# Loads, fills and stores of the first batch laid out anew, and router logits computed turned, in an attention and mixture-of-experts kernel

## The reference, cut to what matters

```python
x = x + attn(layernorm(x));  x = x + ffn(layernorm(x))

# attn
Q, K, V = (x @ W + b for ...)                       # 16 heads of 16
attn = softmax(causal(Q @ K.T) * scale)             # exact maximum per row
h = layernorm(x @ dp_w1 + dp_b1) * ln_g + ln_b      # 128 wide
drift = gelu(h) @ dp_w2 + dp_b2
gate = tanh(gelu(drift * g_w1 + g_b1) @ g_w2 + g_b2)  # one number per token
out = (attn * gate) @ V ... @ Wo + bo

# ffn, 8 experts of 128, 2 chosen per token, and a shared part of 2 x 128
logits = x @ gate_w.T;  scores = sigmoid(logits)    # group-limited choice of 2
y = sum over chosen experts of w2 @ (silu(w1 @ x) * (w3 @ x)) * weight;  + shared(x)
```

## Time and profile before

| | |
|---|---|
| runs | 1950.63, 1959.01, 1960.4 us; median 1959.01 |
| profiled execution, its span | 1949.71 us, 1947.7 us |
| PE matmul, busy | 1735.7 us, 89% |
| PE weight load, busy | 1069.2 us, 55% |
| DVE, ACT, POOL, busy | 67%, 56%, 39% |

### The profile page before, as it was taken

One profiled execution on the slowest core, in us unless ns is written; L12 is line 12 of the kernel. 1 busy time (PEld: TensorE's weight loads), 2 busy tenths in 40 slices (PEclk: granted clock), 3 DMA queues, 4 the chain that ended last, 5 costly groups with the idle time before them and its releaser, 6 DMA issues.

```text
span 1947.7 us, 39672 instructions
## 1 busy us (share of the span) xinstructions
PE 1735.7 (89%) x13066; PEld 1069.2 (55%) x13066; DVE 1302.9 (67%) x2546; ACT 1094.8 (56%) x1822; POOL 763.4 (39%) x1110
## 2 busy tenths in 40 slices
PE   3489889979999899988999899989999889988997
PEld 1244446535665556545665456645665456646786
DVE  1387676866678666866768666776668667763564
ACT  1436755565555754567555774567555665566342
POOL 4422422262115732177214752166321772155151
PEclk8679899979999999989999799998999889988999
DMA  7555353354435555356445464355552563336131
GB/s 237 171 130 141 99 164 99 97 150 118 130 92 164 165 145 155 104 160 187 130 131 157 131 188 122 101 172 150 153 148 86 168 184 100 93 104 191 48 110 41
DMA packets 194881, 263.67 MB, mean 135 GB/s; under 512 B 19712, under 2 KB 129408, under 8 KB 194688
## 3 DMA queue, kind: packets, MB, share of 16 engines
q1 hardware_dynamic: 183936, 231.77, 40.8%
q0 software_dynamic: 10752, 29.37, 5.3%
HBM read 134.13 MB, written 126.35 MB: 134 GB/s over the span
## 4 chain that ended last, share of the span: by engine, by line
PE 61%; DMA 10%; issue 7%; ACT 7%; DVE 6%; POOL 5%; SPq 4%; POOLq 0%; ACTq 0%; DVEq 0%
PE ps_all L1634 12%; PE ps_all L1728 12%; PE ps_all L1582 7%; PE ps_all L1754 6%; PE ps_all L1614 6%; DMA qk_s<-ql 4%; PE ps_all L1566 4%; ACT probs L1137 4%; DVE mx L1282 3%; PE ps_all L1552 3%; PE ps_all L1642 3%; PE ps_all L1667 2%; PE ps_all L1738 2%; PE ps_all L1689 1%; PE ps_all L1589 1%
## 5 line engine op out<-in xcount | busy, mean ns | idle before, releaser
L1282 DVE TENSOR_REDUCE mx<-ps_all 128x2 f32<-128x1024 f32 (+2 forms) x640 | 619.9, 1004 | 124.9 <-PE ps_all L1582 67.4
L1137 ACT ACTIVATE probs<-ps_all 128x1024 f32<-128x1024 f32 x576 | 574.4, 1027 | 214.7 <-PE ps_all L1614 209.6
L1582 PE MATMUL ps_all<-k_st,q_st 48*128 48x512 f32 (+3 forms) x1536 | 309.9, 430 | 71.4 <-DVE mx L1282 22.1
L1634 PE MATMUL ps_all<-probs,vaug 128*32 128x512 f32 (+3 forms) x3072 | 339.6, 538 | 24.0 <-POOL probs L984 16.3
L984 POOL TENSOR_SCALAR_AFFINE_SELECT probs<-probs 128x512 f32<-128x512 f32 x256 | 161.4, 645 | 488.5 <-ACT probs L1137 487.5
L1614 PE MATMUL ps_all<-q_st,k_st 49*128 49x512 f32 (+3 forms) x1536 | 266.5, 401 | 35.5 <-ACT probs L1137 20.5
L1582 PEld LDWEIGHTS ps_all<-k_st,q_st 48*128 48x128 f32 x1536 | 160.0, 197 | 196.9 <-issue 81.4
L1614 PEld LDWEIGHTS ps_all<-q_st,k_st 49*128 49x128 f32 x1536 | 136.1, 194 | 157.7 <-issue 69.6
L1728 PE MATMUL ps_all<-w_hi,x2h 128*128 (+1 forms) x528 | 190.8, 361 | 9.4 <-DVE x2l L1331 4.7
L1728 PE MATMUL ps_all<-w_lo,x2h 128*128 (+1 forms) x528 | 176.4, 334 | 0.0
L1728 PE MATMUL ps_all<-w_hi,x2l 128*128 (+1 forms) x528 | 175.7, 333 | 0.0
(11 more groups left out here) (162 smaller groups left out, 3041.2 us busy)
## 6 DMA issues: line engine op xcount, KB each, us to landing
qk_s<-qh SPq DMA_DIRECT2D x128, 256.0 KB
q_st<-qk_s SPq DMA_DIRECT2D x128, 192.0 KB, 4.1
k_st<-qk_s SPq DMA_DIRECT2D x128, 192.0 KB, 4.8
xs<-xs_s SPq DMA_DIRECT2D x84, 256.0 KB
ys_s<-ysb SPq DMA_DIRECT2D x84, 256.0 KB
qk_s<-ql SPq DMA_DIRECT2D x64, 256.0 KB
o_s<-o_sb SPq DMA_DIRECT2D x64, 256.0 KB, 3.3
xa<-in_x SPq DMA_DIRECT2D x32, 256.0 KB, 3.2
```

Of the source, the lines that this page charges most:

```text
L1137: nc.scalar.activation(to, of, ACT.Exp, scale=DH ** -0.5).then_inc(freed[release[item][0]], 1)
L1282: last = nc.vector.tensor_reduce(to[:, :, p, qt % QPC], both[:, :, at:at + keys], X_AXIS, ALU.max)
L1582: last = mm(bank(item, j)[:, to:to + keys], q_st[r, q_half(n, g, c), p, qt % QPC * P:(qt % QPC + 1) * P], k_st[r, k_half(n, g, kc), p, 0:k ...
L1634: last = mm(bank(first)[32 * h:32 * h + 32, q0 - c * CHUNK:], vaug[:, kt, g, h * VW:h * VW + 32], probs[:, s % 2, h, at:at + cols], start= ...
```

## The change

- SP loads the first two parts of x first; the weights are two items (`WL` 0 for values, `WL` 1 for queries and keys), the small constants and `Wo` an item `WC`, `turn_bars` an item `BT`.
- The fill with ones of `k_st` is cut into five items on POOL (`PK` 0 to 4), that of `vaug` and the small constants are two more; so the normalisation of x can run between them.
- The zeros of the slots are written in 12 transfers of 512 KB (`XZ`), planned from 100,000 ns on, one each 20,000 ns. The six loads of expert weights are planned from 110,000 ns on, one each 20,000 ns, and not earlier (`early`).
- In batch 0 each unit v has its own place for the high and the low part (tiles of later stages, still free, are borrowed) and its own semaphore `first_st[v]`. Only the second half of the batch waits for the stores of the first.
- `CG` holds `gate_w` (128 by 8) as weights and moves 256 tokens: 6 matmuls for a quarter. The logits come out turned, 8 by 256. `CI` takes their tanh on ACT into `logits_t`, `CJ` turns it back on PE with two transposes, and `RT` becomes a copy. The wait for the routing of the batch before moves from `CG` to `RT`.
- Planned lengths and landing times for batch 0 are made smaller, and `FIRST` is 50,000.

```diff
-FIRST = 75_000
+FIRST = 50_000
...
             add("SP", ("AX", n, h), ISSUE, due - 12000, [("AN", n - (h < 2), (h - 2) % HALVES * QT + QT - 1)],
-                lands=4500)
+                lands=4500 if n else 2600)
+            if n == 0 and h < 2:
+                add("SP", ("WL", h), 1800, due, lands=3000)
...
-                    before = [("SQ",) + unit(i - 1)] if i else []
-                    if i > 1:
-                        before.append(("SQ",) + unit(i - 2))
+                    before = [("SQ",) + unit(i - k) for k in ((1, 2) if n else (4,)) if i >= k]
...
-        add("PE", ("CG", n, q), 1400, pre + 14000, low + [("RO", n - 1, ROUTE_OPS - 1)], 1, FULL)
-        add("ACT", ("RT", n, q), 200, pre + 14000, [("CG", n, q)], frees=(("CG", n, q), None))
+        add("PE", ("CG", n, q), 750, pre + 14000, low, 1, FULL)
+        add("ACT", ("CI", n, q), 390, pre + 14000, [("CG", n, q), ("CJ",) + prev])
+        add("PE", ("CJ", n, q), 250, pre + 15000, [("CI", n, q)], 0, FULL)
+        add("ACT", ("RT", n, q), 200, pre + 15000, [("CJ", n, q), ("RO", n - 1, ROUTE_OPS - 1)], frees=(("CG", n, q), None))
...
-        add("SP", ("WF", i), ISSUE, 60000 + 9000 * i, [("WP", i - 1)], lands=5500)
-        add("ACT", ("WH", i), 1300, 60000 + 9000 * i, [("WF", i)])
-        add("POOL", ("WP", i), 2900, 60000 + 9000 * i, [("WH", i)])
+        begin = 110_000 + 20_000 * i
+        add("SP", ("WF", i), ISSUE, begin, [("WP", i - 1)], lands=5500, early=begin)
+        add("ACT", ("WH", i), 1300, begin + 6000, [("WF", i), ("WC",)])
+        add("POOL", ("WP", i), 2900, begin + 8000, [("WH", i)])
+
+    def constants():
+        for k in range(K_HALVES + 2):
+            ns, due = (1000, 5000 + 1500 * k) if k < K_HALVES else (2400, 25000) if k == K_HALVES else (2200, 30000)
+            add("POOL", ("PK", k), ns, due, early=5500 if k < K_HALVES else due)
+        add("SP", ("BT",), 1300, 6000, lands=3000, early=5000)
+        add("SP", ("WC",), 3400, 14000, lands=4000, early=14000)
+        for k in range(2 * CLEARS):
+            begin = 100_000 + 20_000 * k
+            add("SP", ("XZ", k), ISSUE, begin, [("PK", K_HALVES + 1)], lands=6000, early=begin)
...
+        def high_of(n, v):
+
+            if n or v < 2:
+                return qh[:, v % 2, :]
+            return xs[:, v % 2, :, :].rearrange("p t e -> p (t e)").bitcast(F32R)
+
+        def low_of(n, v):
+            if n or v == 0:
+                return ql[:]
+            place = rr[:] if v == 3 else yab[:, v - 1, :, :]
+            return place.rearrange("p a e -> p (a e)").bitcast(F32R)
...
                 for kind in range(2):
-                    sp.wait_ge(qh_st[kind], done * 32)
+                    if n:
+                        sp.wait_ge(qh_st[kind], done * 32)
+                    else:
+                        sp.wait_ge(first_st[2 * m + kind], (c + 1) * 48)
                     fence(sp)
...
+                for k in range(KE):
+                    for t, (xx, w) in enumerate(((x2h, gw_hi), (x2h, gw_lo), (x2l, gw_hi))):
+                        last = mm(bank(item)[0:EXPERTS, 0:Q], w[:, k, :], xx[:, buf, k, :],
+                                  start=(k == 0 and t == 0), stop=(k == KE - 1 and t == 2))
+                last.then_inc(cg_full, 1)
+
+            def turn_logits(item, n, q):
+                pe.wait_ge(cg_tanh, n * QS + q + 1)
                 for i in range(QT):
-                    ts = slice(i * P, (i + 1) * P)
-                    for k in range(KE):
-                        for t, (xx, w) in enumerate(((x2h, gw_hi), (x2h, gw_lo), (x2l, gw_hi))):
-                            last = mm(bank(item)[:, i * EXPERTS:(i + 1) * EXPERTS], xx[:, buf, k, ts], w[:, k, :],
-                                      start=(k == 0 and t == 0), stop=(k == KE - 1 and t == 2))
-                last.then_inc(cg_full, 1)
+                    last = nc.tensor.transpose(bank(("CG", n, q))[:, Q + i * EXPERTS:Q + (i + 1) * EXPERTS],
+                                               logits_t[0:EXPERTS, i * P:(i + 1) * P], ident[0:EXPERTS, 0:EXPERTS])
+                last.then_inc(cj_full, 1)
```

More of the change, by code:

```diff
@@ L68 @@
 FFN_CHUNKS = 6
+CLEARS = 6
 HALVES = TILES // QT
@@ L153, in __init__, with add @@
     def __init__(self):
-        self.items, self.queues, self.place, self.spaced = {}, {}, {}, {}
-    def add(self, engine, item, ns, due, after=(), banks=0, tiling=None, frees=None, lands=None, spaced=None):
+        self.items, self.queues, self.place, self.spaced, self.early = {}, {}, {}, {}, {}
+    def add(self, engine, item, ns, due, after=(), banks=0, tiling=None, frees=None, lands=None, spaced=None, early=0):
         self.items[item] = (engine, ns, due, [a for a in after if a in self.items], banks, tiling, frees, lands)
+        self.early[item] = early
         if spaced and spaced[0] in self.items:
@@ L301, in gate @@
         add("ACT", ("GC", n), 2300, due, [("GB", n)])
-        add("POOL", ("GD", n), 4800, due, [("GC", n)])
+        add("POOL", ("GD", n), 4800, due, [("WC",), ("GC", n)])
         add("ACT", ("GE", n), 3600, due, [("GD", n)])
@@ L312, in values @@
     def values(n, g):
-        add("POOL", ("VA", n, g), 2000, at(n, g) - 4000, [("GL", n), ("PV", n - 1, g, NSTEP - 1)])
+        add("POOL", ("VA", n, g), 2000, at(n, g) - 4000, [("PK", K_HALVES), ("GL", n), ("PV", n - 1, g, NSTEP - 1)])
     def maxima(n, g):
@@ L439, in routing @@
         for i in range(2 * TILES):
-            add("POOL", ("SX", n, i), 1250, begin + 14000 + 500 * i, [("RO", n, INDEX_OP)], lands=4000,
+            add("POOL", ("SX", n, i), 1250, begin + 14000 + 500 * i, [("RO", n, INDEX_OP)] + [("XZ", n * CLEARS + k) for k in range(CLEARS if n < 2 else 0)], lands=4000,
                 spaced=(("SX", n, i - 1), SCATTER_APART))
@@ L455, in pair @@
         expert(n, QS, u, due, [("XO", n, u), ("RO", n, TILE_OP)])
-        add("ACT", ("YC", n, u), 600, due + 3500, [("ED", n, QS, u)] + ([("YS",) + divmod(k - 1, SLOT_PAIRS)] if k else []),
+        add("ACT", ("YC", n, u), 600, due + 3500, [("ED", n, QS, u)] + ([("YS",) + divmod(k - 1, SLOT_PAIRS)] if k else [("XZ", 2 * CLEARS - 1)]),
             frees=(("ED", n, QS, u), None))
@@ L488, in rest @@
             pair(n, u)
+    constants()
     for n in range(B):
@@ L641, in build @@
         qh_st = [sem(f"qh_st{i}") for i in range(2)]
+        first_st = [sem(f"first_st{i}") for i in range(2 * KE)]
         g_dve, g_pool, g_act, g_mean = sem("g_dve"), sem("g_pool"), sem("g_act"), sem("g_mean")
@@ L907, in _, with constants @@
             nc.gpsimd.tensor_copy(bars[:, 0, 1, :], causal).then_inc(bars_set, 1)
[L908 to L917 removed]
+            def constants(item, k):
+                if k < K_HALVES:
+                    nc.gpsimd.memset(k_st[:, k, :, :].bitcast(F32), 1.0).then_inc(ones_set, 1)
+                elif k == K_HALVES:
+                    nc.gpsimd.memset(vaug[:], 1.0).then_inc(ones_set, 1)
+                else:
+                    nc.gpsimd.memset(ysb[:, 0, :], 0.0).then_inc(ones_set, 1)
+                    for i in range(EXPERTS):
+                        nc.gpsimd.memset(fills[:, i:i + 1], float(i * P))
+                    for i in range(SLOT_TILES):
+                        nc.gpsimd.memset(tile_no[:, i:i + 1], float(i))
+                    for one in scan:
+                        nc.gpsimd.memset(one[:, 0:PAD, :], 0.0)
+                    nc.gpsimd.memset(ones[:], 1.0).then_inc(ones_set, 1)
             def rstd_a(item, n, h):
@@ L1006, in scatter_tile @@
                 pool.wait_ge(route, routed(n, INDEX_OP))
-                if n == 0:
-                    pool.wait_ge(xs_clear, 32)
-                elif n >= 2:
+                if n < 2:
+                    pool.wait_ge(xs_clear[n], CLEARS * 16)
+                else:
                     for b in range(2):
@@ L1189, in copy_slots @@
                 if k == 0:
-                    act.wait_ge(xs_clear, 32)
+                    for i in range(2):
+                        act.wait_ge(xs_clear[i], CLEARS * 16)
                 else:
```

141 lines of the change are left out of this document (76 added, 65 removed).

## The result

Twenty runs of the kernel after have a median of 1939.15 us (1926.96 to 1956.09), twenty of the kernel before 1950.62 (1942.7 to 1960.4). The ratio is 0.9939, 95% interval 0.9918 to 0.9959: faster by 12 us, clear of noise but well under 2%. The prediction, a ratio of 0.972 and 1904 us, was wrong: some 43 us of the forecast gain didn't come, and the time lies above its range of 1884 to 1934. The profiled execution took 1940.05 us (span 1938.3).

The account below looks back on a forecast made before the run. PE was taken as the bound, after a beginning under half load: 1949.7 - 50 (beginning) - 9.6 (logits) + 5 (zeros, expert weights) = 1895.1 us profiled, ratio 0.972, median 1904; range 1884 to 1934.

Parts of the forecast that it names:

- PE starts at 7.3, second statistics before 6: Start of the kernel: PE begins 3.65 us after x at 3.63; DVE does the second statistics before 6 us.
- I take 50: Beginning, up to batch 0's first sums: 50 us saved of a computed 54, bounds 28 to 54.
- rival A: Beginning stays half serial: 15 to 20 us lost, first sums at 81 to 86, median 1919 to 1924; chance 0.17.
- The marker: Batch 0's first sums (first `PV`), at 120 us before, forecast at 66; taken as the same state in both kernels.
- From there on PE is full: After the first `PV` at 120.04 us PE is full, so that time was taken as the marker.
- Logits, -9.6: Gate logits on PE: 0.40 us saved for each of 32 quarters, 12.8 us, three quarters counted; bounds -12.8 and 0.
- rival B: Start is won, but waits replace PE's saved logits work: logits 0, median 1914, up to 1930; chance 0.08.
- I take three quarters: Share of the 12.8 us saved on PE's logits counted to the end, from chain share 61% and load 92%.
- Zeros and expert weights, +5: Both moved under batch 0's attention: cost of 5 us together, as DMA and POOL are more than half idle.
- rival C: `WF` loads hold SP in the attention, waiting for `WP`: at 12 us each of six, median 1971; chance 0.04.
- Due times, 0, 10 each way: Smaller `FIRST` moves all later due times alike: cost 0, with 10 us each way for the order made anew.
- The other 1828 us stay 92% busy: Rest of the kernel after the first 120 us: PE's load there stays 92%, as before.

Follow-up runs that it names:

- e2: Kernel after with the turned logits undone (logits computed as before), on two chips: 0.9923 and 0.9946 of the kernel before.
- e6: Kernel after with the expert weight loads back at their old, early due times: 0.9928 of the kernel before.
- e5: Kernel after with batch 1's x loaded from 62 us, batch 0's stores planned to land in 7 us, its gate due earlier: 0.9935 and 0.9916 of the kernel before.
- e10: Kernel after with the six logits matmuls of each quarter done twice, same order: 0.9987 of the kernel before.
- e3: Kernel after with the zero transfers planned later, from 265 us on, 8 us apart: 0.9971 of the kernel before.
- e11: e5, turned logits kept, but planned at the old logits' length of 1400 ns: 0.9907 of the kernel before.
- e8: e5 with the old logits in place of the turned ones, timed three times: 0.9833, 0.9863 and 0.9892 of the kernel before.
- e12: e8, old logits kept, but planned at the new logits' length of 750 ns: 0.988 of the kernel before.
- e4: Kernel after with 28 filler matmuls on PE in its wait for the second half's stacks: 0.9924 of the kernel before.

## Why the prediction was wrong, by its own steps

- **PE starts at 7.3, second statistics before 6:** right, 7.71, and all four at 3.83 to 5.3.
- **"I take 50" for the beginning:** this step failed, in two ways. First in its parts. PE's projection work was taken without gaps, to 42, and the data to be ready by 61; DVE stood behind x of batch 1, a store of SP's landed in 9.7, and the last stacks of that stage came at 59.2 with their maxima still to do. The gate went behind maxima: rival A, with first sums at 85.2 as it had it (81 to 86), though its time, 1919 to 1924, was wrong too. The marker moved by 34.8, within the bounds of 28 to 54, and at 85.2 it is just past the 85 that the prediction named as a sign of being wrong; a landing of low parts is still on the chain. Then in its meaning: "From there on PE is full" made each us of the marker a us of the end. Of 34.8 there were 14.1 left at the first sums of batch 1, and 10 to 15 at the end (e2). The work that had stood idle at a low clock now ran at that low clock (17.7 us), and no term of the sum had the clock in it. e6 moved the marker by 13 with no effect at the end, e5 moved the next one by 9 to 17 with almost none.
- **Logits, -9.6:** the matmuls were sized right (0.40 us saved a quarter, 12.8 in all; from start to next start it is 26.8 + 7.1 = 33.9 us for 32, where it was 46.9 before, 13.0 less) and `CJ` hardly waits, as forecast. The worth was wrong: 0 here, as rival B had it, and a loss in the repaired start, which nothing had. The step that failed is that the saving at the logits was taken for a saving of PE: of 12.5 us at one clock 4 are left in PE's sum, and that is less than these timings can tell from nothing. Rival B had waits in the place of saved work; the waits only moved. "I take three quarters" isn't refuted by e10, which gives half, with 2 to 19 us of 22.7.
- **Zeros and expert weights, +5:** nearer to 0. No wait of SP for `WP` is seen in the kernel after, rival C had nothing; e3 and e6 won nothing by moving them.
- **Due times, 0, 10 each way:** nothing speaks against it. `FIRST` at 65,000 (e9) changed nothing, and kernels that differ in one planned length only (e5 and e11, e8 and e12) are about 3 us apart, within the scatter.
- **"The other 1828 us stay 92% busy":** 1526 + 159 of 1853 us behind the first sums, 91%. One point there is 19 us, and a busy share at a low clock isn't work done.
- Sum by what was measured, to the end: start -14 at batch 1, of which -10 to -15 is left at the end (e2 twice: 0.9923, 0.9946), logits 0, the rest 0. That is the 12 us measured.

The range failed since its high end, 1934, like the worst case behind it, 1936 by the prediction's own sum, had the worst start and 0 for the logits and then still counted every us of the marker.

## What to carry to other kernels

Before a gain at the start is counted to the end, look for a second marker later on and ask what the engines do between the two: idle time at a low clock that is filled with work at that low clock is won only by half. A saving on the busiest engine is to be looked for in that engine's whole work, at one clock and each us counted once: here a third of it was left, and it gave nothing. Try each part of a change alone, and together with the next one: without its turned logits this one, with the order of the start repaired, was 0.4 to 1% faster than as it was made, though either step taken alone gave nothing that shows.

## What the runs showed of the hardware

- PE's granted clock was at its lower level from 56.5 to 100.9 us, after PE had been idle since 51.5, and stayed there with PE busy 71%, then 91% by the rows. In e4 it fell at 67.8, 3 us behind 12.25 us in which PE was busy without a gap at 1.00. The Trainium skill, "TensorE: Matmul & The Clock Gate", its part on the clock gate, has the clock follow how busy PE has been; the rows of the filler agree; those of 78 to 101 us don't, if busy is read off the matmul rows. What kept the clock low there wasn't settled.
- Time goes with the mean granted clock of a run. Of the kernel after, a run at 0.939 took 1926.96 us, one at 0.923 1951.23; over the twenty runs it is 1.4 us for 0.001. Sets in which the kernel before ran at a mean of 0.919 to 0.921 gave it medians of 1991 to 2000 us, those at 0.929 to 0.932 1949 to 1955. By 1.4 us for 0.001 the clock explains 15 of the 42 us between the two sets on one chip number. PE's idle time differs too: e8 has 165.8 us of it in a set of the second kind, 191.5 and 196.1 in sets of the first. What makes the sets differ is open.
- A 256 KB store took 9.7 us from issue to landing between 41 and 51 us, with the DMA share at 0.59, when SP had issued stores and loads almost without a gap; the planner had 2.6.
- In the kernel before, the load of x that SP issued right behind the two fills of 3072 KB took 8.61 us to issue; the load just before them took 0.37.
